# A macaron block on one core: places of the first FFN one step earlier, 71 expert blocks instead of 72, other waits in attention's first steps

## The reference

```python
x = x + 0.5 * ffn(layernorm(x))
x = x + attention(layernorm(x))
x = x + 0.5 * ffn(layernorm(x))

def ffn(x):        # 8 experts of inner size 352, the best 2 of each token; one shared of 176
    top_v, top_i = top_k(x @ gate_w, 2)
    combine = softmax(top_v) scattered to the 8 experts
    d = (silu(x @ Wg[e]) * (x @ Wu[e])) @ Wd[e]          # for each expert e
    return sum_e combine[:, e] * d[:, e] + (silu(x @ Sg) * (x @ Su)) @ Sd

def attention(x):  # 16 heads of size 8, linear attention with running sums over time
    q, k, v = split(x @ W_attn + b_attn);  q, k = elu(q) + 1, elu(k) + 1
    kv, ksum = cumulative sums over t of k[t] v[t]^T and of k[t]
    y = (q . kv) / (q . ksum + 1e-6)
    return y @ W_proj + b_proj
```

## Time and profile before

| | us |
|---|---|
| median of 3 runs (lowest to highest) | 1247.82 (1246.77 to 1250.56) |
| the profiled execution, its own time | 1248.63 |
| its span, first to last instruction | 1246.6 |
| tokens of the first FFN | 0 to 200.5 |
| experts of the first FFN | 200.5 to 457 |
| attention and tokens of the second FFN | 457 to 952 |
| experts of the second FFN | 952 to 1211 |
| last combination and stores | 1211 to 1246.6 |

### The profile page before, as it was taken

One profiled execution on the slowest core, in us unless ns is written; L12 is line 12 of the kernel. 1 busy time (PEld: TensorE's weight loads), 2 busy tenths in 40 slices (PEclk: granted clock), 3 DMA queues, 4 the chain that ended last, 5 costly groups with the idle time before them and its releaser, 6 DMA issues. The chain is left out here.

```text
span 1246.6 us, 32188 instructions
## 1 busy us (share of the span) xinstructions
PE 999.2 (80%) x9076; PEld 750.5 (60%) x9077; DVE 900.7 (72%) x2377; ACT 673.8 (54%) x1474; POOL 846.9 (68%) x878
## 2 busy tenths in 40 slices
PE   2667655999999937788988898888864999999940
PEld 1444334899989924455555555555433899898940
DVE  6778783666766744788888888888854666666748
ACT  5556642555555623466666555666431555555545
POOL 4677773777777844467787787878642777777850
PEclk8889986999999967999999999999976999999975
DMA  9311121222222211001111111100003222222229
GB/s 280 104 49 49 54 85 55 79 77 76 82 75 76 74 56 34 17 29 42 34 34 35 49 36 38 42 19 17 20 33 82 77 78 77 78 74 77 73 89 332
DMA packets 69023, 86.89 MB, mean 70 GB/s; under 512 B 13164, under 2 KB 56625, under 8 KB 68974
## 3 DMA queue, kind: packets, MB, share of 16 engines
q1 hardware_dynamic: 51566, 52.41, 14.5%
q0 software_dynamic: 17408, 33.87, 8.2%
HBM read 45.01 MB, written 43.30 MB: 71 GB/s over the span
## 5 line engine op out<-in xcount | busy, mean ns | idle before, releaser
L489 POOL DMA_INDIRECT expert_results<-ey,eidx x288 | 299.6, 1040 | 70.8 <-issue 64.8
L481 POOL DMA_INDIRECT routed_rows<-row,idx x256 | 253.4, 990 | 73.6 <-issue 71.1
L1128 DVE SCALAR_TENSOR_TENSOR ehT<-eh,ehT 128x768 f16<-128x768 f32 x144 | 138.0, 958 | 151.6 <-ACT ehT L681 151.6
L676 ACT ACTIVATE esil<-PSUM 128x768 f32<-128x768 f32 x144 | 116.8, 811 | 236.3 <-PE PSUM L815 226.7
L813 PE MATMUL PSUM<-eT,WGU 128*128 128x256 f16 x864 | 237.7, 275 | 1.2
L814 PE MATMUL PSUM<-eT,WGU 128*128 128x256 f16 x864 | 237.4, 275 | 0.0
L815 PE MATMUL PSUM<-eT,WGU 128*128 128x256 f16 x864 | 237.4, 275 | 0.0
L503 POOL TENSOR_TENSOR space<-qk,val 128x1152 f32<-128x1152 f32 x64 | 138.3, 2172 | 73.7 <-DVE shift L1178 52.5
L813 PE MATMUL PSUM<-WD,ehT 128*128 x864 | 164.0, 221 | 7.8 <-DVE ehT L1128 5.2
L814 PE MATMUL PSUM<-WD,ehT 128*128 x864 | 162.6, 221 | 0.1
L815 PE MATMUL PSUM<-WD,ehT 128*128 x864 | 162.1, 220 | 0.0
(11 more groups left out here) (197 smaller groups left out, 2306.2 us busy)
## 6 DMA issues: line engine op xcount, KB each, us to landing
xe<-routed_rows SPq DMA_DIRECT2D x144, 130.0 KB
space<-expert_results SPq DMA_DIRECT2D x32, 512.0 KB, 4.1
expert_results<-ey,eidx POOLq DMA_INDIRECT x288
X<-in_L_attn_x_dram SPq DMA_DIRECT2D x16, 256.0 KB, 4.7
routed_rows<-row,idx POOLq DMA_INDIRECT x256, 2.3
out_dram<-X SPq DMA_DIRECT2D x16, 256.0 KB, 4.4
routed_rows<-pad_rows SPq DMA_DIRECT2D x24, 130.0 KB
space<-in_L_ffn_Wg_dram SPq DMA_DIRECT2D x1, 1408.0 KB, 9.1
```

The lines of the kernel that those rows point to most:

```text
L481: pool.indirect_dma_start(routed, bass.IndirectOffsetOnAxis(ap=idx[u][:, k, j:j + 1], axis=0), row[u][:, j, :], None).then_inc(s_scattered ...
L489: pool.indirect_dma_start(result, bass.IndirectOffsetOnAxis(ap=eidx[u][:, h:h + 1], axis=0), ey[u][:, h, :], None, bounds_check=K * T - 1, ...
L676: act.activation(esil[u][:, :], PSUM[:, 1536 * u:1536 * u + 768], ACT.Silu, scale=2.0 ** -(SX + SWT)).then_inc(s_block_silu, 1)
L1128: return dve.scalar_tensor_tensor(out=dst, in0=src, scalar=float(2 ** scale), in1=high, op0=ALU.mult, op1=ALU.subtract)
```

## The change

Four edits. In both expert phases the 72nd block is left out on all engines; each engine gives the semaphore steps of that block by a drain instead, and the waits for the results' DMAs count 36 and 35 blocks instead of 36 and 36. In the first FFN `place(n+1)` stands in step n behind `row_low(n+2)` (for n = 0, behind `choose(1)`) instead of at the head of step n+1. In attention, group 1's deviations come in step -2 right behind its moments instead of at the head of step -1; and GpSimd doesn't wait for deviations in steps -1 and 0.

```diff
             def load_block(f):
                 def step(n, v):
+                    if isinstance(n, int) and n == (f + 1) * NBLK - 1:
+                        sp.wait_ge(s_block_rows[v], (n - v) * (16 // XE))
+                        sp.drain().then_inc(s_block_rows[v], 16)
+                        return
...
             def results(n, u):
+                if isinstance(n, int) and n in (NBLK - 1, 2 * NBLK - 1):
+                    pool.drain().then_inc(s_carrier, 1)
+                    return
                 pool.wait_ge(s_block_results, n + 1)
...
                         if attend:
-                            pool.wait_ge(s_deviations, m + (NG + 3))
+                            if not isinstance(m, int) or m > 0:
+                                pool.wait_ge(s_deviations, m + (NG + 3))
                             outer(m + 1, 1, 0)
...
                 for u in range(2):
-                    pool.wait_ge(s_results[u], 16 * HALVES * NBLK // 2 * (f + 1))
+                    pool.wait_ge(s_results[u], 16 * HALVES * (NBLK // 2 - u) * (f + 1))
...
-                with act.Fori(0, (NBLK - 4) // 2) as i:
+                with act.Fori(0, (NBLK - 6) // 2) as i:
                     step(i * 2 + (n0 + 4), 0)
                     step(i * 2 + (n0 + 5), 1)
-                hi(n1 - 1, 1)
+                step(n1 - 2, 0)
+                hi(n1 - 2, 0)
+                results(n1 - 3, 1)
                 results(n1 - 2, 0)
-                results(n1 - 1, 1)
+                act.drain().then_inc(s_block_silu, 1)
+                act.drain().then_inc(s_block_high, 1)
+                act.drain().then_inc(s_block_results, 1)
...
-                for m in range(2 + (NBLK - 4) // PASS * PASS, NBLK):
-                    step(m, m % XE, e, turn=m < NBLK - 1, read=m < NBLK - 1)
+                for m in range(2 + (NBLK - 4) // PASS * PASS, NBLK - 1):
+                    step(m, m % XE, e, turn=m < NBLK - 2, read=m < NBLK - 2)
+                block_down(n1 - 3, 1, e[1])
                 block_down(n1 - 2, 0, e[2])
-                block_down(n1 - 1, 1, e[3])
+                pe.drain().then_inc(s_block_turned, 1)
+                pe.drain().then_inc(s_block_products, 1)
+                pe.drain().then_inc(s_block_out, 1)
...
-                step(n1 - 2, 2)
-                step(n1 - 1, 3, ahead=False)
-                block_low(n1 - 1, 1)
+                step(n1 - 2, 2, ahead=False)
+                block_low(n1 - 2, 0)
+                dve.drain().then_inc(s_block_T, 1)        # and three more drains
...
             def first_ffn(n, v, i=None, b=None):
-                place(n, v, n)
                 if edge and n == 0:
+                    place(0, 0, 0)
                     deviations(3, 1, 4)
...
                 if not edge or n < NG - 1:
                     choose(n + 1, (v + 1) % 4, n + 1)
                 if edge and n == 0:
+                    place(1, 1, 1)
                     moments(1, 5)
                 if not edge or n < NG - 2:
                     row_low(n + 2, (v + 2) % 4)
+                if not edge or 0 < n < NG - 1:
+                    place(n + 1, (v + 1) % 4, n + 1)
...
-                if route or ready:
+                if (route or ready) and not (isinstance(m, int) and m == -1):
                     deviations(1)
...
                 if ready and not (isinstance(m, int) and m == NG - 3):
                     dve.wait_ge(s_combined, m + 4)
                     moments(1, m + 3)
+                    if isinstance(m, int) and m == -2:
+                        deviations(1)
```

More of the change, by code:

```diff
@@ L411, in _ @@
                 for u in range(2):
-                    sp.wait_ge(s_results[u], 16 * HALVES * NBLK // 2 * (f + 1))
+                    sp.wait_ge(s_results[u], 16 * HALVES * (NBLK // 2 - u) * (f + 1))
                 if f == 0:
@@ L693, in res_value @@
             def res_value(n, u):
-                return (n - u) * (16 * HALVES // 2)
+                return (n - u) * (16 * HALVES // 2) - 16 * HALVES * u * ffn[0]
             def experts(f):
@@ L1311, in experts @@
                         step(i * XE + (n0 + 2 + b), (2 + b) % XE)
-                step(n1 - 2, 2)
-                step(n1 - 1, 3, ahead=False)
-                block_low(n1 - 1, 1)
+                step(n1 - 2, 2, ahead=False)
+                block_low(n1 - 2, 0)
+                dve.drain().then_inc(s_block_T, 1)
+                dve.drain().then_inc(s_block_hidden, 1)
+                dve.drain().then_inc(s_block_low, 1)
+                dve.drain().then_inc(s_block_places, 1)
             def combine_first(g):
```

## The result

| kernel | median us (lowest to highest, runs) | ratio to before, 95% interval |
|---|---|---|
| before | 1247.90 (1245.22 to 1250.56, 20) | |
| changed | 1245.70 (1242.67 to 1248.67, 20) | 0.9979 [0.9971, 0.9988] |

The change makes the kernel 2.6 us faster (1247.9 x 0.0021; 1.5 to 3.6 by the interval), not 9.6. The profiled execution took 1244.23 us with a span of 1242.5 us, against 1248.63 and 1246.6 before.

The account below looks back on a forecast made before the run. PE was taken to bound the expert phases, GpSimd the first FFN, one chain through DVE, PE, ACT and GpSimd attention's first steps. Blocks -6.7, places -2.9, drains 0, attention 0: -9.6 us from 1247.82, so 1238.2; range 1233 to 1243.5.

Parts of the forecast that it names:

- 71 blocks: Both expert phases: dropping the last block saves one block's 3.35 us in each, 6.7 us in all.
- its fill and its run-down [...] stay the same, one block earlier: Expert phases: the dropped block comes from the pipeline's steady part, so each phase loses the full 3.35 us.
- Drains: Ends of the expert phases: the stand-in drains cost 0, bounds 0 to +1.5 us, as the barrier's second drain is short.
- The bound for the second phase: Behind the second expert phase: if drains add up, 0.9 of 1.5 us late is covered and 0.6 lost.
- Places: First FFN: earlier placing cuts GpSimd's waits, 2.9 us won; bounds 8.8 us won to 2 us lost.
- Attention: Attention's first steps: early deviations and dropped waits give 0; bounds 1.6 us won to 1 lost.
- the third waits: Group 1's early deviations: the third operation is held beside GpSimd's products until 477.2, the next until 479.4.
- pushes the first product of attention (and PE's sums behind it) by 0.5: Attention step -1: features(0, 1) starts 2.3 us late, ends at 481.9, and delays that product by 0.5.
- the division: Attention step 0: it waits for the last 1.2 us of GpSimd's product, 0.85 us late with 0.3 counted.
- a sign of being wrong: Attention: the sums of the old 514.26 moving by over 1 us against the barrier before them.
- Places win nothing: Rival: in the first FFN DVE's lateness meets GpSimd's gain, leaving -6.7 us, 1241.1; with or without drains, chance 0.23.
- under 3.7 us with losses in several places: Case: result within 3.7 us, as the block's time doesn't go or losses come in several places; chance 0.06.

Follow-up runs that it names:

- f4_68: The kernel before with 68 blocks in each FFN, leaving out 22 rows in the second expert phase; 1225.58 us, 0.9833 of the kernel before.
- e4_wait0: The changed kernel with GpSimd's wait for deviations kept in step 0, left out in step -1 alone; 1245.59 us, 0.9977 of the kernel before.
- i3_changed: The changed kernel run once more, for a second value of the whole; 1245.70 us, 0.9994 of the kernel before.
- f2_dev_only: The kernel before with group 1's deviations right behind its moments in step -2, GpSimd's waits kept; 1251.68 us, 1.0042 of the kernel before.
- f1_blocks_places: The changed kernel with attention as it was: 71 blocks and places one step earlier; 1241.92 us, 0.9965 of the kernel before.
- e1_blocks: The kernel before with only the edits of the 72nd block; 1243.93 us, 0.9972 of the kernel before.
- e2_places: The kernel before with only the places one step earlier; 1245.50 us, 0.9986 of the kernel before.
- e3_attention: The kernel before with only the two attention edits, early deviations and no GpSimd waits in steps -1 and 0; 1252.30 us, 1.0037.

## Why the prediction was wrong

*71 blocks, -6.7 forecast; -3.5 (-2.1 to -5.0) measured alone, -4.9 in the traces.* The block's time is right: from first to last silu the first phase takes 234.7 us with 72 blocks and 231.4 with 71, the second 235.3 and 232.1 (means of five traces each). (The 3.35 us of the earlier trace rows hold one interval of 4.97; the others average 3.32.) The step that failed is "its fill and its run-down [...] stay the same, one block earlier", and it failed in the first phase alone. There the mean run-down is 11.05 us with 72 blocks and 12.87 with 71, and the phase lost 1.5 us in place of 3.35. The second phase has 11.3 and 11.05, and lost 3.4. The difference is the copy of block 69, held by a late completion of block 67's DMAs. The earlier trace rows cover the steady part, and the end of the phase was taken over from the kernel before without a look at what its copies wait for. The held copy accounts for 1.8 of the missing 3.2 us; the rest is within the interval of the time.

*Drains, 0.* Right, and by the reason given: one long drain, then one of 53 ns. The next phase's first combination operation stands 4.90 us behind the last DMA against 4.86. The size of the long one was off, 4.5 us for 2.67. That it also takes in the landing of the DMAs, which the phase waits for in any case, is likely and not shown. The bound for the second phase used 3.33 us of the earlier trace rows for the drain at 1207.5; that drain took 2.67.

*Places, -2.9 forecast; -1.7 measured alone, and no gain at the phase's end in the traces.* The waits behaved nearly as worked out. Forecast tickets 30.1, 41.3 and 56.0; the five other profiled kernels with early places have 30.0 to 30.4, 41.5 to 41.9 and 56.0 to 56.5, with the wait of 4.4 us at group 3 (4.5 was forecast). Group 6, forecast at 87.6, came at 88.8 to 89.3. GpSimd waited 6.1 to 7.7 us in the six kernels with early places, 8.8 to 10.0 in the seven without (6.7 and 9.2 in the mean, so 2.5 us of waits were won). The step that failed is that its own work stays what it was, a term put at nothing without a reason: from group 1's ticket to the last scatter, waits taken off, it is 159.1 to 159.9 us with early places and 156.9 to 157.5 without, 2.6 us more in the mean. In the repeated run of the changed kernel 2.2 of that are tickets. Timelines of POOL and of DVE there:

```profile
77.70 1.13 POOL L482 TENSOR_TENSOR ticket<-ones 128x1 f32<-128x1 f32 x1
```
```profile
77.91 0.88 DVE L1143 SCALAR_TENSOR_TENSOR WGU<-space,WGU  x1
```

The ticket ends 0.04 us behind DVE's product of two SBUF operands. With `place` moved that product comes beside the ticket; in the kernel before it ran beside an indirect DMA's issue (74.94 us beside 75.25). So the last scatter ends at 195.95 to 197.64 us in the six, at 195.88 to 197.25 in the seven. That the time alone still shows -1.7 (-0.6 to -2.9) is not explained by these traces. In the profiled execution of the changed kernel one cause more is seen: the ticket of group 3 came 1.3 us or more later than in the others (57.80), as DVE was late.

*Attention, 0 forecast (+1 at worst); +4.6 measured alone, +1.8 to +3.6 in the changed kernel.* The kind of cost was named, its size was not. Three steps failed.

First, "the third waits", since only operations of two SBUF operands were counted: the first two of the ten, of one operand each, were held (0.96 and 2.06 us).

Second, "pushes the first product of attention (and PE's sums behind it) by 0.5": `features(0, 1)` ended nearly where forecast (481.65, or 482.2 in the old times, as GpSimd's first product stands 0.58 earlier; 481.9 forecast), and the sums came 0.8 us later for 0.5. But PE stood idle for 3.59 us ahead of them, and what follows differs from trace to trace. In this execution it ran them at full clock (0.70 and 1.02 us again) and the third `features` came as in the kernel before. In the repeated run, behind 3.81 us of idle time, the same sums took 0.82 and 1.92 us and the third `features` came 1.7 us later. The forecast had no term for the clock.

Third, the division: forecast 0.85 us late because two SBUF operands meet the last 1.2 us of GpSimd's product; in fact its first operation (one operand, 0.22 us before) met the product at its start and took 2.23. That cost 1.5 to 2.1 us in each of the four kernels with it, and the granted clock in 498 to 510 us is 0.86 for 1.00. The sums of the old 514.26 came 1.5 us later behind the phase's first combination operation, 2.8 in the repeated run; over 1 us was a sign of being wrong.

The sixth `features` of the phase stands 1.95 to 3.32 us later behind that operation than in the kernel before in the three profiled kernels with all attention edits, and 1.9 us earlier to 0.1 later in the six others with none. Compared with those six too, the loss is 2 to 5 us.

The Trainium skill ("SBUF — State Buffer", the shared port pair) states the lock for a DVE operation with two SBUF inputs and also for one in a 2-port performance mode. I had used the first half alone. The traces agree that one-operand operations are held for GpSimd's whole product (2.06 and 2.23 us beside one of 2.17); in which mode they ran, no row shows.

*Rivals.* "Places win nothing" (-6.7) was nearest in kind and still too high; no rival had the run-down or an attention loss of this size. What came, under 3.7 us with losses in several places, had been given 0.06. The traces put the terms at -4.9 for -6.7, 0 for -2.9, and some 2 to 5 us for attention's 0, which is the largest miss.

## To carry to other kernels

When a pipeline is made one step shorter, its end is another stretch of code beside other transfers: here one late completion of 16 reached a wait on one of two buffers, which had been met in time before, and two more small buffers took it out of the way. Ask of the end what each wait there waits for, and don't explain it by what the work is worth; the packet sizes in the trace tell which blocks are empty. Before moving DVE operations into a gap, look at what GpSimd does in that gap, whatever the number of operands; an idle engine is not free time if its neighbour holds it. And where an engine's waits shrink, read its work again: a hold that moves from one engine's instruction to another's shows as a longer duration and not as a wait.

## What the runs showed of the hardware

- At the phases' ends a GpSimd drain took 2.0 to 4.6 us behind indirect DMAs (2.02 in `f4_68`) and 53 ns when it is repeated with none issued between.
- An indirect DMA of 128 rows has 16 completions. In the nine phases with a held copy 15 of them stand within 0.2 us, and the sixteenth comes 1.5 to 2.2 us later, with a 16 KB packet of the queue "instruction" beside it.
- DVE operations of one SBUF operand (128x8 and 128x64, fp32 and int32) took 0.96, 2.06 and 2.23 us instead of 0.17 to 0.22 beside GpSimd's product of 2.17.
- A GpSimd product of one element for each partition took 1.12 to 1.15 us instead of 0.2 beside DVE's product of 0.88 us with two SBUF operands.
- In two of the five sets of runs all kernels stood at 1.13 times their usual time, on chips that ran at the usual level in another set, with the excess shown as idle "issue". Ratios to the kernel before, taken beside it, did not all carry over: 0.9891 for 0.9965 in one kernel.
- PE's sums ran at its lower clock level behind 2.23, 3.81 and 4.22 us of idle time (`e4_wait0`, `i3_changed`, `f2_dev_only`), and at the higher one behind 1.54 and, in the changed kernel's first trace, 3.59. The length of the idle time alone doesn't decide it.
- Single executions differ in the clock of short stretches. In a stretch of 10 us in the last attention step of `f1_blocks_places` it was 0.66 (first fence), in the changed kernel 1.00, and the last two tickets stood 3.3 and 3.6 us further behind the one before them:

```profile
897.00:907.00 10.00, 7.44 (x23) 4.22 (x24) 5.19 (x6) 0.45 (x1) 7.57 (x9) 0.66 0.12 41
```
```profile
896.00:906.00 10.00, 6.70 (x23) 3.73 (x22) 7.41 (x9) 3.67 (x7) 7.60 (x8) 1.00 0.06 21
```

From the last ticket but two to the next it is 22.7 to 22.9 us in the six traces with 1.00 there, 24.3 in the three with 0.83 (`e1_blocks`, `e2_places`, `e4_wait0`) and 26.2 to 26.3 in the four with 0.66 (`e3_attention`, `f2_dev_only`, `f4_68`, `f1_blocks_places`). That is as much as a whole edit here, so phases of one trace each can't be compared for 2 us. `e3_attention` and `f2_dev_only` have the low clock there, and their times (+4.6 and +5.2 us) may hold part of it: one trace each can't tell whether it goes with the edit.
